# Two sets of expert lists, full-height bias products, and the two linear layers as one chain in the last block of a transformer kernel

## The reference

```python
x = x + gelu(h @ w_ff1 + b_ff1) @ w_ff2 + b_ff2          # h = layer_norm(x), 128 -> 512 -> 128
return x @ w_d + b_d                                      # added to the residual before it

probs = softmax(xf @ router_w.T)                          # 8 experts, the best 2 of each token
probs = probs * mask
probs = probs / (probs.sum(-1) + 1e-09)
g = xf @ gate_w[e] + gate_b[e]
u = xf @ up_w[e] + up_b[e]
h = silu(g) * u                                           # 256 hidden
expert_out = h @ down_w[e] + down_b[e]
y = sum over e of probs * expert_out                      # and x = x + y
```

## Time and profile before

| | |
|---|---|
| median of 3 runs | 1830.43 us (1828.17 to 1834.92) |
| profiled execution: time, span | 1829.23 us, 1827.4 us |
| mean granted clock | 0.811 |
| TensorE busy | 1366.6 us (75%) |
| VectorE busy | 1188.4 us (65%) |
| ScalarE busy | 774.9 us (42%) |
| GpSimd busy | 380.1 us (21%) |
| last block: chunks | from 1424 to 1574 us |
| last block: table, weights, waits | 1574 to 1595 us |
| last block: tiles | 1595 to 1801 us |
| last block: end | 1801 to 1827.4 us |

### The profile page before, as it was taken

How to read it: one execution, slowest core, us unless ns; L and a number is a source line. 1 busy time by engine, 2 the same in 40 slices (tenths; PEclk the granted TensorE clock), 3 DMA queues, 4 the chain that set the end, 5 groups by cost and what they waited for, 6 DMA issues and landing times. The chain is left out here.

```text
span 1827.4 us, 29827 instructions
## 1 busy us (share of the span) xinstructions
PE 1366.6 (75%) x9389; PEld 761.1 (42%) x9389; DVE 1188.4 (65%) x2853; ACT 774.9 (42%) x1045; POOL 380.1 (21%) x528
## 2 busy tenths in 40 slices
PE   4689999999989999999868226500276687399994
PEld 2344444443434444443446115400154466266662
DVE  3568889988978888897068843248664544524445
ACT  1113777776767777778733000000142322123331
POOL 0311111111111111100121025411410355413332
PEclk9865999998989999999988555555587888559997
DMA  2001111111110100112001034354000000111114
GB/s 60 0 0 42 43 43 43 43 43 43 43 44 34 46 19 32 42 43 79 28 23 51 19 91 111 87 211 144 15 1 1 7 32 31 41 30 50 53 52 147
DMA packets 64534, 89.71 MB, mean 49 GB/s; under 512 B 11122, under 2 KB 43356, under 8 KB 64395
## 3 DMA queue, kind: packets, MB, share of 16 engines
q1 hardware_dynamic: 57483, 74.90, 12.0%
q0 software_dynamic: 6912, 13.02, 2.9%
HBM read 42.07 MB, written 47.52 MB: 49 GB/s over the span
## 5 line engine op out<-in xcount | busy, mean ns | idle before, releaser
L710 DVE TENSOR_REDUCE mx<-psum 128x1 f32<-128x512 f32 x1024 | 630.9, 683 | 89.9 <-PE psum L558 89.0
L665 ACT ACTIVATE probs<-psum 128x1024 f32<-128x1024 f32 x512 | 518.8, 1025 | 176.1 <-PE psum L582 170.1
L558 PE MATMUL psum<-akT,aqT 32*128 32x512 f32 x1024 | 398.2, 536 | 12.5 <-DVE mx L710 7.7
L598 PE MATMUL psum<-probs,vaug 128*32 128x256 f32 x4096 | 336.7, 409 | 0.1
L582 PE MATMUL psum<-aqT,akT 32*128 32x512 f32 x1024 | 264.6, 511 | 9.3 <-DMA aqT<-mT 5.0
L558 PEld LDWEIGHTS psum<-akT,aqT 32*128 32x128 f32 x1024 | 177.8, 196 | 74.8 <-DVE mx L710 54.9
L582 PEld LDWEIGHTS psum<-aqT,akT 32*128 32x128 f32 x1024 | 98.4, 188 | 221.0 <-issue 162.9
L598 PEld LDWEIGHTS psum<-probs,vaug 128*32 128x32 f32 x4096 | 86.7, 111 | 128.2 <-issue 77.0
L299 POOL TENSOR_TENSOR scaled<-qkv,qscale 128x256 f32<-128x256 f32 x16 | 9.8, 615 | 593.6 <-ACT akT L650 593.5
L2015 POOL DMA_INDIRECT pair_rows<-yo,dest x72 | 70.4, 978 | 143.5 <-DVE dest L2432 137.3
L1606 PE MATMUL psum<-ident,h 128*128 128x128 f32 x32 | 5.3, 292 | 124.4 <-DVE h L743 124.4
(11 more groups left out here) (315 smaller groups left out, 2137.0 us busy)
## 6 DMA issues: line engine op xcount, KB each, us to landing
slot_rows<-pads SPq DMA_DIRECT2D x33, 520.0 KB, 3.9
pick_rows<-zeros SPq DMA_DIRECT2D x48, 256.0 KB, 2.1
yk<-pick_rows SPq DMA_DIRECT2D x8, 1536.0 KB, 9.1
xg<-slot_rows SPq DMA_DIRECT2D x72, 65.0 KB, 1.8
token_rows<-xrow SPq DMA_DIRECT2D x8, 512.0 KB, 2.8
XO<-pair_rows SPq DMA_DIRECT2D x8, 512.0 KB, 4.8
w1b<-in_w1T SPq DMA_DIRECT2D x8, 352.0 KB, 4.5
w3b<-in_w3T SPq DMA_DIRECT2D x8, 352.0 KB, 5.2
```

Source lines behind the costliest of these rows:

```text
L558: last = e.matmul(bank[:], qT[u % NG][r, i * P:(i + 1) * P], kT[u % NG][r, c * 512:(c + 1) * 512], start=True, stop=True)
L598: last = e.matmul(ctxp[h * R:(h + 1) * R, q], vaug[g][:, kt, h, :], probs[:, (2 * k + h // 2) % SLOTS, h % 2, q], start=(kt == 0 and part ...
L665: a.activation(probs[:, n % SLOTS, :, :], scores[:, n % 2, :, :], ACT.Exp)\
L710: dve.reduce_max(mx[:, h, i, c:c + 1], bank[:], X_AXIS).then_inc(tp_free, 1)
```

## The change

- The lists are made in LS = 2 sets: tokens of chunks 0 to 3 fill the first, those of chunks 4 to 7 the second, each with its own counts, table of TPS = 39 tiles and region of `slot_rows`. The tile loop runs over 78 tiles. SyncE waits only for the sends of a set before its tiles.
- The last seven groups of sends (two DMAs each) stand on GpSimd's queue between the first results of the tile loop (the first stands before it). The pairs of chunks 0 to 3 are loaded (SyncE, at tiles 58, 63, 68, 73) and added (VectorE, at tiles 65, 69, 73, 77) within the loop.
- `one2` and `brow` have 128 partitions, of which all but two are zero: the bias products are 128 rows high.
- wf2 times wd is formed once (`wfd`); one product `product(c)` adds XO^T wd and f wfd in one bank. `sums`, `add_sums` and `back` go; transposes of XO (`turn_sources`) and their copies come.
- `turn_rows`, `logits`, `ranks`, `pick`, `places` and `send` come one iteration later. GpSimd has `rstd(c-2)` ahead of `send(c-4)`, VectorE has `add_product(c-2)` first.

The core of the diff:

```diff
-TILES = 72
+LS = 2
+TPS = (2 * B * S // LS - E1) // P + E1
...
-        brow = sb("brow", [2, BROW * E1], F32R)
-        one2 = sb("one2", [2, P], F32R)
+        brow = sb("brow", [P, BROW * E1], F32R)
+        one2 = sb("one2", [P, P], F32R)
...
+            def result_in(c):
+
+                if c % CPS == 0:
+                    for i in range(YB):
+                        sp.wait_ge(yout[i], 16 * used((c // CPS + 1) * TPS, YB, i))
                 if c >= 4:
                     sp.wait_ge(both_r, (c - 3) * CH)
                     sp.dma_start(out[c - 4], X[:, (c - 4) * CH:(c - 3) * CH, :]).then_inc(st, 16)
                 sp.dma_start(yk[:, c % 4, :, :], pairs[c]).then_inc(yld[c % 4], 16)
+
+            for s in range(LS):
+                for i in range(RB):
+                    sp.wait_ge(scat[i], OUT_ROWS * ((s + 1) * CPS // RB))
+                sp.wait_ge(town, (s + 1) * TABLE_STEPS)
+                for j in range(TPS):
+                    if s and j >= TPS - 20 and (j - TPS + 20) % 5 == 0:
+                        result_in((s - 1) * CPS + (j - TPS + 20) // 5)
+                    load_tile(s, j)
+            for c in range((LS - 1) * CPS, NC):
+                result_in(c)
...
-            pool.memset(f32(one2[:]), 1.0).then_inc(one_r, 1)
+            pool.memset(f32(one2[:]), 0.0).then_inc(one_r, 1)
+            pool.memset(f32(brow[:]), 0.0).then_inc(one_r, 1)
+            pool.memset(total[:], 0.0).then_inc(one_r, 1)
+            pool.wait_ge(one_r, 3)
+            pool.memset(f32(one2[0:2, :]), 1.0).then_inc(one_r, 1)
             pool.wait_ge(cb_r, 1)
...
-            for c in range(NC + 3):
-                if 0 <= c - 3:
-                    send(c - 3)
-                if 0 <= c - 1 < NC:
-                    rstd(c - 1)
...
+            for c in range(NC + 2):
+                if 0 <= c - 2 < NC:
+                    rstd(c - 2)
+                if 0 <= c - 4:
+                    for k in range(CH):
+                        send(c - 4, k)
+            last = [(c, k) for c in range(NC - 2, NC) for k in range(CH)]
+            for n in range(ALL_TILES):
+                if LS == 1:
+                    while last:
+                        send(*last.pop(0))
+                elif last:
+
+                    send(*last.pop(0))
+                result_out(n)
...
             def turn_rows(c):
                 e.wait_ge(rown, c + 1)
 
-                e.wait_ge(yts, c + 1)
+                e.wait_ge(xots, min(c + 4, NC))
+                if c:
+                    e.wait_ge(rts, c)
...
+            def product(c):
+
+                bank = ps[5 + 2 * (c % 2)]
                 e.wait_ge(gl, (c + 1) * NF)
...
+                    e.matmul(bank[:, ks], xoT[:, c % 2, ks], wd[:], start=True, stop=False)
                     for n in range(NF):
...
+                        last = e.matmul(bank[:, ks], f[:, c % 2, n, ks], wfd[:, n * D:(n + 1) * D],
+                                        start=False, stop=(n == NF - 1))
                 last.then_inc(d1, 1)
 
             turn(0)
...
+            turn_sources(0)
+            for n in range(NF):
+                last = e.transpose(ps[5][:, n * P:(n + 1) * P], wf2[:, n, :], t["ident"][:])
+            last.then_inc(w2turned, 1)
+            e.wait_ge(rep_r, 1)
+            e.matmul(ps[7][:, 0:D], bf2rep[:], wd[:], start=True, stop=True).then_inc(cbm, 1)
+            for c in range(NC + 4):
+                if c == 3:
+                    e.wait_ge(ld10, LOADED10)
+                    e.wait_ge(one_r, 4)
+                if 0 <= c - 3 < NC:
+                    turn_rows(c - 3)
                 if c < NC:
                     hidden(c)
...
                 if 0 <= c - 3 < NC:
-                    ranks(c - 3, c)
+                    logits(c - 3, c)
+                if 0 <= c - 4 < NC:
+                    ranks(c - 4, c)
                 if 0 <= c - 1 < NC:
-                    sums(c - 1)
-                if 0 <= c - 2 < NC:
-                    logits(c - 2, c)
+                    product(c - 1)
                 if c + 1 < NC:
                     turn(c + 1)
...
-            for c in range(NC + 3):
+            dve.wait_ge(begun, 1)
+            for c in range(NC + 4):
+                if 0 <= c - 2 < NC:
+                    add_product(c - 2)
                 if c + 1 < NC:
                     normalise(c + 1)
                 if c == 0:
                     split_biases()
-                if 0 <= c - 3:
-                    places(c - 3)
-                if 0 <= c - 1 < NC:
-                    add_sums(c - 1)
+                if 0 <= c - 4 < NC:
+                    places(c - 4)
+                if 0 <= c - 3 < NC:
+                    pick(c - 3)
                 if 0 <= c - 2 < NC:
-                    pick(c - 2)
-                if 0 <= c - 1 < NC:
-                    add_product(c - 1)
-                    normalise_rows(c - 1)
+                    normalise_rows(c - 2)
...
+            for l in range(LS):
+                table(l)
...
+                if n + 2 < ALL_TILES:
+                    low(n + 2)
+                if LS > 1 and n >= ALL_TILES - 16 and (n - ALL_TILES + 16) % 4 == 3 and n < ALL_TILES:
+                    add_pairs((LS - 2) * CPS + (n - ALL_TILES + 16) // 4)
+            for c in range((LS - 1) * CPS, NC):
+                add_pairs(c)
```

More of the change, by code:

```diff
@@ L2056, in turn_rows, with logits @@
                 last.then_inc(rturned, 1)
+            def logits(c, at):
+                e.wait_ge(rts, c + 1)
+                if c:
+                    e.wait_ge(pown, (c - 1) * PICK_STEPS + 1)
+                e.wait_ge(gl, min((at * NF + 1), NC * NF))
+                for k in range(CH):
+                    last = e.matmul(ps[1][:, k * E1:(k + 1) * E1], xfT[:, k * P:(k + 1) * P], rw[:],
+                                    start=True, stop=True)
+                last.then_inc(lgm, 1)
             def ranks(c, at):
@@ L2270, in _ @@
+            for n in range(ALL_TILES + 1):
+                if n < ALL_TILES:
+                    silu(n)
+                if n:
+                    hidden_rows(n - 1)
+                if n + 2 < ALL_TILES:
+                    high(n + 2)
         @block.vector
@@ L2468, in _ @@
                                                  op0=ALU.mult, op1=ALU.add).then_inc(done, 1)
+            for n in range(2):
+                low(n)
+            for n in range(ALL_TILES + 2):
+                if n < ALL_TILES:
+                    hidden(n)
+                if 0 <= n - 2:
+                    result(n - 2)
+                if n + 2 < ALL_TILES:
+                    low(n + 2)
[3 more added lines that the diff above has]
+                add_pairs(c)
 def network(nc, t):
```

447 lines of the change are left out of this document (209 added, 238 removed).

## The result

The changed kernel takes **1748.7 us** (median of 4 runs, 1743.7 to 1784.5; the profiled one 1747.11, span 1745.3, mean granted clock 0.829). Run beside it, the kernel before took 1829.3 (1807.0 to 1834.9): a ratio of 0.959, interval 0.948 to 0.970. Two later comparisons of the same two kernels gave 0.963 (0.961 to 0.966) and 0.963 (0.957 to 0.969); the kernel before against itself gave 0.999 (0.993 to 1.005). One and the same kernel has slower executions, some per cent longer, and the ratios leave these out.

What follows compares the result with a forecast made beforehand. It took chained chunk iterations, a TensorE gap, a TensorE-bound tile loop and VectorE's final additions as limits; -19.5 up to the loop, -3.4 in it and -8 after took 1829.2 to 1798.3, plus 1.2: 1799.5 us, range 1789 to 1822.

Steps and rivals of the forecast that it cites:

- the part on the loop: Tile loop: six more tiles +15.2 us, less time at 1.2 GHz -18.6, bias height otherwise nothing; together -3.4 us.
- The clock: Start of the tile loop: with full-height bias products 7 us at 1.2 GHz instead of 49.8, worth -18.6 us.
- Rival 1: Tile loop: bias rows did not keep the clock down, about 50 us at 1.2 GHz stay; 1818 us, chance 0.17.
- Rival 3: Tile loop: the clock stays low far into it; slower, 1872 us with 39 tiles at 4.49 us, chance 0.07.
- The lead of the result buffers: Sends between the first eight results: four result buffers give a lead of ten tiles, so nobody waits, 0 us.
- The pair additions in the loop: VectorE's four pair additions inside the tile loop: 0 to 0.5 us each, taken as 0.
- The chunks: Chunk iterations 3 to 6: 13.5 us each instead of 14 to 19; chunk 7's hidden product at 1513, against 1521.30.
- The opening: Start of the block: +3 us from added TensorE work and slower normalising, +1.5 from GpSimd's fill (bounds 0 and +4.7).
- rival 2: Chunk iterations give nothing, the whole -15 us up to the count is lost; 1814.5 us, chance 0.11.
- Between: From the count to the first tile product: two tables +2.4 us, no wait for the last sends -6.9 us.
- the end: After the loop: half the pair additions gone -8.4 us, stores sharing the queue +0.4; -8 us.
- Rival 4: Pair loads or sends hold the loop, or last loads and stores fill the queue: +8, 1807.5 us, chance 0.04.

Runs made afterwards that it cites:

- e5: Changed kernel with the bias table and ones 32 rows high instead of 128; 1802.6 us, 0.991 of the kernel before.
- e11: Changed kernel with two-row bias products, the two of a tile issued side by side; 1797.2 us, one run.
- c1: The changed kernel itself, run again for comparison on another chip; 1747.5 us, 0.963 of the kernel before.
- e10: Changed kernel without the two bias products of each tile (those biases missing from the result); 1758.6 us, one run.
- e6: Changed kernel with the bias table and ones 64 rows high instead of 128; 1816.8 us, one run.
- e7b: Second run of the kernel before with GpSimd's reciprocal root ahead of the eight sends in each chunk; 1825.8 us, 0.997 of the kernel before.
- e7: Kernel before with GpSimd's reciprocal root ahead of the eight sends in each chunk, first run; 1819.8 us, 0.990 of the kernel before.
- c2: The kernel before itself, profiled again on another chip; 1842.3 us, ratio 0.999.
- e2: Changed kernel with the bias table and ones two rows high again, the fill kept; 1825.9 us, 0.985 of the kernel before.
- e1: Kernel before with only the bias table and ones made 128 rows high, zero-filled; 1776.1 us, 0.965 of the kernel before.
- e4: Changed kernel with all remaining sends issued ahead of GpSimd's first result transfer; 1762.3 us, 0.957 of the kernel before.
- e12: Kernel of e9 with the bias table's fill cut into four pieces behind the first four roots; 1763.6 us, 0.958 of the kernel before.
- f1: Kernel of e12 with one set of lists instead of two; 1736.7 us, 0.954 of the kernel before.
- f3: The changed kernel itself, run beside f1 and f2 on one chip; 1746.8 us, 0.963 of the kernel before.
- e3: Changed kernel with one set of lists (71 tiles) instead of two; 1747.9 us, 0.947 of the kernel before.
- e9: Kernel of e8 with chunk 6's sends also ahead of the first result, only chunk 7's between results; 1738.4 us, 0.961 of the kernel before.
- f2: The kernel of e9 run again, beside f1 and f3; 1731.5 us, 0.953 of the kernel before.
- e8: Changed kernel with second table and pair weights done one operation after each of the first 28 tiles; 1742.4 us, 0.962 of the kernel before.

## Why the prediction was wrong

**The step that failed** is the sentence on the bias products in the part on the loop: "weight loads of 2 and of 128 rows take 198 and 203 ns, the columns stay, so nothing directly". The durations are right, and they are not the price: the change of height is, 0.32 us for each pair of changes and 0.64 us a tile (e5 and e11 against c1), in a term that stood at nothing. The second half of the same rows showed it: L2160 and L2159 are the two groups of weight loads with 19.9 and 14.8 us of idle time ahead of them "issue", 0.28 and 0.21 us for each of 72. I read the busy column of those rows and not the idle one. With 0.64 us for each of 78 tiles, about 50 us, the sum would have been near 1750. From the idle time of those two rows alone, 0.49 us a tile, it would have been 1761.

The Trainium skill, TensorE: Matmul & The Clock Gate, Part 3, says that weight loads overlap with products in flight only when their row groups differ, and that a load is pulled ahead for another row group or into the background buffer. The runs differ from the first sentence: loads and products of one and the same full height do overlap (the load at 1641.44 within the product from 1641.33), and it is the loads next to a change of height, from 128 to 32 and back, that start 0.17 and 0.25 us late. The second sentence fits the full-height case.

**The clock** was right in size: 5.8 us at 1.2 GHz after the first tile product where 7 stood in the sum, and 50 before. As for the cause, the twelve profiled executions with all of the loop's products at full height agree: the granted clock rises 3 to 6 us after the first tile product. Eleven of them have a mean of 0.89 to 0.98 in the loop's first 50 us, and e10 has 0.72, because its clock fell again when TensorE had been busy for 2.42 of 5 us (windows):

```profile
1583.00:1588.00 5.00, 2.42 (x14) 1.47 (x12) 1.06 (x4) 1.04 (x3) 3.78 (x5) 0.98 0.21 66
1588.00:1593.00 5.00, 1.96 (x7) 1.47 (x8) 0.71 (x3) 0.28 (x1) 3.78 (x5) 0.50 0.16 53
```

In the eight with fewer rows the clock rises after 5 (e6), 10 (e7b), 18 (e11), 28 (e7), 32 (c2), 50 (before, e5) and 55 us (e2). Of these before, e7, c2 and e7b have one and the same loop, and e1 has it at full height and 3 us. So fewer rows go with a longer low stretch, but do not bring it each time. Rival 1 did not come: the transposes stayed, three a tile, and the clock rose. Rival 3 did not come either.

**The lead of the result buffers** failed as a consequence: with the short products four buffers cover the interleaved sends (e2 and e5 have no wait for a result buffer; at least nine of their first twelve tiles take 4.49 us, and no run shows it at 2.54 alone), at 1.90 us a tile they do not: 7.1 us (e4), where 0 stood. **The pair additions in the loop** cost 1.1 us each at three tiles (these take 2.9 to 3.1 us and not 1.90; the fourth comes behind the last gate product), 3.3 us where 0 stood. With 6 x 1.90 = 11.4 for the tiles added, these make 21.8, and -63.6 + 21.8 = -41.8 against the measured -40.7.

**The chunks.** Forecast 13.5 us an iteration, measured 12.38; TensorE waits 0.97 us ahead of `turn_rows` as it was to, but the further 0.9 of small waits were not there. The opening is near its sum of 4.5 us by luck: the first product of the block comes 5.0 us later and the third chunk's 4.0, but the fill holds VectorE's first normalisation throughout, 3.9 us (e12), near the upper bound and not the 1.5 taken, and the rest is 1.1 at the first product and not 3. For this the Trainium skill, SBUF — State Buffer, section "Who interferes with whom", has the rule that VectorE, in a mode that `tensor_scalar` can enter, and GpSimd take a shared port pair for the whole instruction, and that the one issued first blocks the other. The fill was issued 0.04 us earlier (1415.77 against 1415.81), and the trace agrees with that; no row tells the mode of VectorE's operations. Chunk 3 is 1.5 us later than before, to 2.5 forecast. The tail from chunk 7's hidden product was 45.0 us to VectorE's read of the count, to 46 forecast. Up to the count (TensorE's) this is -21.9 us, forecast -15; rival 2 (nothing) is out. Which of the reordered steps owns it stays open (e7, e7b).

**Between** was 1 us better than the -4.5 of the sum (+2.4 - 6.9); **the end** -5.8 from the last down product, -6.7 from SyncE's first DMA after it (1803.98 before, 1728.59 after), to -8 forecast. Rival 4 (+8) did not come as such, though the additions and sends did take 10.4 us of the loop.

**The two sets**, a main part of the change, bring nothing in this form: they save 4.7 us ahead of the loop (6.7 by f1 against f3) and 5.9 at the end and cost 24.2 in it.

## What to carry to other kernels

Where TensorE bounds a loop, compare the start-to-start distances and the idle time ahead of its weight loads, not their durations: a cheap-looking product of another height than its neighbours cost 0.32 us here, and two of them a quarter of a tile's 2.54 us. Fill such operands with zeros to the full height, or put the short products side by side. When a loop gets faster, recount every cover that was worked out at the old pace, queues of GpSimd first; and lay a long GpSimd fill where VectorE is idle.

## What the runs showed of the hardware

- A product of 2, 32 or 64 rows between products of 128 costs the same 0.32 us for going in and out; two such products side by side cost it once (2.55, 2.22 and 1.90 us a tile at a granted clock of 1.00).
- A GpSimd fill of 128x5120 (4.44 us), issued 0.04 us ahead of four VectorE operations of 1.12 us together, stretched them to 5.06 us; laid elsewhere it gave back 3.9 us.
- VectorE's chain of small dependent operations can get gaps of 0.2 to 1.8 us beside GpSimd's indirect DMA issues: 9.7 us for a table of 3.9 (e4). All five executions that have them (e3, e4, e7, e7b, e12) are on the three chips of the next point and have four to six sends beside the table. But six others with four or five sends beside it have none (before, e1, c2, e9, f1, f2), two of them on these chips. The cause is open.
- On three of the five chips TensorE stands still for some 3 to 8 us at a time while no row tells who holds it. In e4, the window row of such a stretch, and VectorE's operation after it, whose products had started 8.7 us and more before (1521.32 the last):

```profile
1523.00:1530.00 7.00, 0.00 (x0) 0.00 (x0) 0.00 (x0) 0.00 (x0) 4.05 (x5) 0.83 0.14 48
...
1530.01 0.69 DVE L2340 TENSOR_TENSOR X<-X,psum 128x512 f32<-128x512 f32 x1 [9.89 <-remote]
```

GpSimd's issues go on meanwhile. Kernels with and without the change had them (c2, e1, e3, e4, e6, e7, e7b, e10, e11, e12, in a smaller size e2); f1 to f3, c1, e5, e8, e9 and the two executions profiled first had none. The cause is open, and so is how much of the 13 to 21 us between the chips is theirs; but this stretch of kernels measured on different chips is not to be compared to within that.
